# A conditioning step computed in two row halves of the TensorE array, and a reordered GpSimd queue

## The chip, the cores and the metric

The kernel runs on one core of one Trainium2 chip. The metric is the device time of one execution in microseconds (us), the median of three runs. The engines are named as in the profile: PE is TensorE (PEld its weight loads), DVE is VectorE, ACT is ScalarE, POOL is GpSimd, SP is SyncE, which here only issues DMAs.

## The reference, cut to what matters

`x` is 32 batches x 32 tokens x 256 features. The first step conditions it: each batch `b` picks a 32x32 matrix and a bias row by its index, and the matrix mixes the 32 tokens.

```
w = weights[subjects]; b = bias[subjects]          # 32 x (32 x 32), 32 x 32
out = jnp.einsum('bct,bcd->bdt', x, w)             # c, d: the 32 tokens; t: the 256 features
out = out + b[:, :, None]
x = x + attention(out, W_qkv, b_qkv, W_out, b_out) # 16 heads, causal
x = x + ffn(lora_ffn(x, ...), W1, W2, W3)          # gate/up/down with adapters, then an FFN with a
                                                   # Walsh-Hadamard transform folded into W2
```

## The kernel before, in words

**Numbers in two parts.** All large products are made of three matmuls in a rounded 32-bit format: high part times high part, low times high, high times low (`both`, lines 383 to 392). So every activation has a `_hi` copy, written by ACT, and a `_lo` copy, the rest, written by DVE or POOL. A product may start only when both copies are there.

**Halves.** The 1024 tokens are two halves `s` of 16 batches. A half is 4 groups `g` of 128 tokens, and a group is 4 batches of 32 tokens, called slots. Features are two chunks `c` of 128.

**The condition step.** DVE builds it in three instructions for each half: `condition_product` (line 880), `condition_sum` (line 886), which leaves each batch's matrix in `cond_sel`, and `condition_blocks` (line 892), which spreads it to a block matrix of 128 x 128 for each group (four 32x32 blocks on the diagonal, zeros elsewhere), 512 columns for a half. `condition_bias` (line 902, two instructions) writes the bias rows. PE then multiplies, for a half and a feature chunk, four groups of 128x128 by 128 columns in plain f32 (`conditioned`, line 406), which the profile shows as two instructions each, and adds the bias by two matmuls with 8 rows (`conditioned_bias`, line 413). Each pair (s, c) has a PSUM bank. ACT copies the bank to `act_hi` (`conditioned_hi`, line 667), DVE writes `act_lo` and so frees the bank (`conditioned_lo`, line 914). `query`, `key` and `v` read both, and wait for chunk 0 ahead of their first three matmuls and for chunk 1 ahead of the next three (line 421).

**Order.** Each engine has its program written out by hand, in order; nothing is planned at run time. On PE: 14 warm-up matmuls, (0,0) with bias, (0,1) with bias, (1,0), (1,1), the two biases of half 1, then `query(0, 0)`, `key(0, 0)` and the rest. On ACT: two weight splits, `conditioned_hi(0, 0)`, then `fold_raw_hi(0, 1, 2)` (line 748), which waits for the DMA of W2, then `conditioned_hi(0, 1)`, `fold_raw_hi(3)`, and half 1. On DVE: the condition step of half 0 and then of half 1, `weights_lo(W_Q)` (line 909), `conditioned_lo(0, 0)`, `conditioned_lo(0, 1)`.

**Later.** The gate/up products of units 0 to 4 are made half by half, those of units 5 to 7 for both halves together. POOL writes the `_lo` parts of the hidden products (`hidden_lo`, line 1179) and of most weights (`weights_lo`, line 1141), and computes the rest of the Hadamard transform of W2 in six `butterflies` (line 1160). In the loop at line 1224, POOL does for m = 0, 1, 2 two butterflies, then `hidden_lo(1, m)` and one `weights_lo`; for m = 3, 4 only the last two. ACT waits for all six butterflies (line 835), writes the high part of the new W2 in four instructions (line 837), and only then goes on with the SiLU of the gates of unit 5 (`gate`, line 737), which frees PSUM banks that PE claims again for unit 7.

Of the kernel before, what the change touches and what calls it, by code (L numbers as in the profile page):

```python
# [47 lines left out]
BH = B // HALVES  # L48
SLOTS = P // T
GROUPS = BH // SLOTS  # L50
DC = D // P
# [6 lines left out]
N, R = 8, 16  # L58
# [13 lines left out]
C_SLOT = C_ODD + 2  # L72
# [8 lines left out]
W_Q, W_K, W_V, W_OUT, W_A, W_GU = 0, 1, 2, 3, 4, 5  # L81
# [28 lines left out]
ALONE = 5  # L110
# [59 lines left out]
def build(nc, index, first, x_slots, w_stream, matrices, w2_t, x_feat, out):  # L170
    with ExitStack() as ctx:
        def sb(name, shape, dt=F32):
            return ctx.enter_context(nc.sbuf_tensor(name, shape, dt))

        def sem(name):
            return ctx.enter_context(nc.semaphore(name))


        const = sb("const", [P, C_END])
# [4 lines left out]
        ones = sb("ones", [N, P], F32R)  # L184
# [25 lines left out]
        act_hi = sb("act_hi", [P, DC, TOK], F32R)  # L210
        act_lo = sb("act_lo", [P, DC, TOK], F32R)
# [4 lines left out]
        q_t, k_x, v_tok, prob, h_hi, h_lo = [], [], [], [], [], []  # L216
# [14 lines left out]
        x_slot = [k[:, 0:GROUPS * D].rearrange("p (g d) -> p g d", d=D) for k in flat_k]  # L231
        cond_prod = [k[:, 1024:2048].rearrange("p (g d n) -> p g d n", d=T, n=N) for k in flat_k]
        cond_all = const[:, C_COND:C_COND + T * N].rearrange("p (d n) -> p d n", n=N)
        fside = const[0:N, C_FSIDE:C_FSIDE + T]
        cond_blk = prob[1][:, 0:2].rearrange("p i r k -> p (i r k)").rearrange("p (g j d) -> p g j d", j=SLOTS, d=T)

        fb_hi, fb_lo = (w[0:N, RING - TOK:RING].rearrange("p (b d) -> p b d", d=T) for w in (w_hi, w_lo))
        idx_slot = index_f[:, 0:NG]
# [2 lines left out]
        slot_of_pair = const[:, C_ODD:C_ODD + 2]  # L241
# [30 lines left out]
        blk_made = sem("blk_made")  # L272
# [4 lines left out]
        xc_hi_made = sem("xc_hi_made")  # L277
# [23 lines left out]
        def tile(name, s, m):  # L301
            return banks[TILES[name, s, m][0]]

        def wait_full(eng, name, s, m):
            bank, before = TILES[name, s, m]
            eng.wait_ge(bank_full[bank], before + 1)

        def full(ins, name, s, m):
            ins.then_inc(bank_full[TILES[name, s, m][0]], 1)

        def free(ins, name, s, m):
            ins.then_inc(bank_free[TILES[name, s, m][0]], 1)

        def wait_read(eng, name, s, m):

            bank, before = TILES[name, s, m]
            eng.wait_ge(bank_free[bank], before + 1)
# [8 lines left out]
        def half(s):  # L326
            return slice(s * HT, (s + 1) * HT)
# [5 lines left out]
        def y_part(s, i, h):  # L333

            return tile("y", s, i)[:, h * 2 * P:(h + 1) * 2 * P].rearrange("p (g n) -> p g n", g=GROUPS)

        def f32(ap):
            return ap.bitcast(F32)

# [28 lines left out]
        def _(pe):  # L368
            def claim(name, s, m):
                bank, before = TILES[name, s, m]  # L370
                if before:
                    pe.wait_ge(bank_free[bank], before)
                return banks[bank]

            def weights(n):
                wait_weights(pe, n)
                at = PLACES[n][0]
                return w_hi[:, at:at + COLS[n]], w_lo[:, at:at + COLS[n]]
# [19 lines left out]
                return [(h_hi[s][:, k, :], h_lo[s][:, k, :]) for s in ss]  # L398


            def conditioned(s, c):
                ps = claim("xc", s, c)
                pe.wait_ge(blk_made, s + 1)
                pe.wait_ge(x_loaded[s], 16)
                for g in range(GROUPS):
                    pe.matmul(ps[:, g * P:(g + 1) * P], x_slot[s][:, g, c * P:(c + 1) * P],  # L406
                              cond_blk[:, s * GROUPS + g], start=(g == 0), stop=False, skip_group_check=True)

            def conditioned_bias(s, c):
                pe.wait_ge(ones_made, 1)  # L410
                pe.wait_ge(fbias_made, 2 * (s + 1))
                for fb in (fb_hi, fb_lo):
                    last = pe.matmul(tile("xc", s, c)[:, :], ones[:, :], fb[:, s * BH:(s + 1) * BH, :], start=False,  # L413
                                     stop=fb is fb_lo, skip_group_check=True)
                full(last, "xc", s, c)

            def projected(name, n, s, m):
                w = weights(n)
                ps = claim(name, s, m)
                for c in range(DC):  # L420
                    wait_read(pe, "xc", s, c)
                    last = both([ps], unit(w, m * DC + c), rows(act_hi, act_lo, c, [s]), c == 0, c == DC - 1)
                full(last[0], name, s, m)

# [5 lines left out]

            def v(s, j):
                w = weights(W_V)
                for c in range(DC):
                    wait_read(pe, "xc", s, c)
                ps = claim("v", s, j)
                for g2 in range(2):
                    for c in range(DC):
                        at = s * HT + (2 * j + g2) * P
                        x_hi, x_lo = act_hi[:, c, at:at + P], act_lo[:, c, at:at + P]
                        wv = [a[:, c * D:(c + 1) * D] for a in w]  # L440
                        o = ps[:, g2 * D:(g2 + 1) * D]
                        pe.matmul(o, x_hi, wv[0], start=(c == 0), stop=False)  # L442
                        pe.matmul(o, x_hi, wv[1], start=False, stop=False)  # L443
                        last = pe.matmul(o, x_lo, wv[0], start=False, stop=(c == DC - 1))  # L444
                full(last, "v", s, j)
# [88 lines left out]
            pe.wait_ge(warm_made, 1)  # L534
            for _ in range(WARM_UP):
                pe.matmul(banks[7][:, :], warm[:, 0:P], warm[:, :], start=True, stop=True)
            conditioned(0, 0)
            conditioned_bias(0, 0)
            conditioned(0, 1)
            conditioned_bias(0, 1)  # L540
            conditioned(1, 0)
            conditioned(1, 1)
            conditioned_bias(1, 0)
            conditioned_bias(1, 1)
            query(0, 0)
# [60 lines left out]
            for name, n in (("d0", W_D0), ("zd", W_AD), ("d1", W_D1)):  # L606
                w = weights(n)
                tiles = down[name] = [claim(name, s, 0) for s in range(HALVES)]
                for k in range(HC):
                    pe.wait_ge(prod_split, SPLIT_COUNT["up", 1, k])  # L610
                    last = both(tiles, unit(w, k), h_rows(k), k == 0, name == "zd" and k == HC - 1)
# [5 lines left out]
            for s in range(HALVES):  # L617
                for m, name in enumerate(("d0", "d1")):
                    last = both([down[name][s]], unit(w, m), rows(aux_hi, aux_lo, 0, [s]), False, True)
# [18 lines left out]
            for js in ([0, 1], [2], [3], [4]):  # L638
                tiles = [claim("w2", j, 0) for j in js]
                for k in range(HC):  # L640
                    pe.wait_ge(prod_split, SPLIT_COUNT["f3", 1, k])
                    m = OUTS[js[0]][0]
# [3 lines left out]
                    last = both(outs, w, xs, k == 0, k == HC - 1)  # L646
# [5 lines left out]
        def _(act):  # L652
# [9 lines left out]
                act.activation(w_hi[:, at:at + COLS[n]], raw[:, n % STAGES, 0:COLS[n]], ACT.Copy)\  # L662
                   .then_inc(w_hi_made, 1)

            def conditioned_hi(s, c):
                wait_full(act, "xc", s, c)
                act.activation(act_hi[:, c, half(s)], tile("xc", s, c)[:, :], ACT.Copy).then_inc(xc_hi_made, 1)

            def queries(s, m):
                wait_full(act, "q", s, m)  # L670
# [194 lines left out]
        def _(dve):  # L865
# [23 lines left out]
            def condition_blocks(s):  # L889
                g = slice(s * GROUPS, (s + 1) * GROUPS)  # L890
                dve.wait_ge(sel_made, s + 1)
                dve.tensor_tensor(cond_blk[:, g], cond_sel[:, g].unsqueeze(2)
                                  .to_broadcast([P, GROUPS, SLOTS, T]),
                                  const[:, C_SLOT:C_SLOT + SLOTS].unsqueeze(1).unsqueeze(3)
                                  .to_broadcast([P, GROUPS, SLOTS, T]), ALU.mult).then_inc(blk_made, 1)

            def condition_bias(s):
                b = slice(s * BH, (s + 1) * BH)
# [10 lines left out]
                dve.tensor_tensor(w_lo[:, at:at + COLS[n]], raw[:, n % STAGES, 0:COLS[n]],  # L909
                                  f32(w_hi[:, at:at + COLS[n]]), ALU.subtract).then_inc(w_lo_first, 1)  # L910

            def conditioned_lo(s, c):
                dve.wait_ge(xc_hi_made, DC * s + c + 1)
                free(dve.tensor_tensor(act_lo[:, c, half(s)], tile("xc", s, c)[:, :],
                                       f32(act_hi[:, c, half(s)]), ALU.subtract), "xc", s, c)

            def constants():
                dve.tensor_tensor(k_bias[:, :, :], const[:, B_K:B_K + DC].unsqueeze(2).to_broadcast([P, DC, 4]),
# [218 lines left out]
        def _(pool):  # L1137
            def weights_lo(n):
                at = PLACES[n][0]
                pool.wait_ge(w_hi_made, n + 1)  # L1140
                pool.tensor_tensor(w_lo[:, at:at + COLS[n]], raw[:, n % STAGES, 0:COLS[n]],  # L1141
                                   f32(w_hi[:, at:at + COLS[n]]), ALU.subtract).then_inc(w_lo_made, 1)
# [38 lines left out]
            def hidden_lo(s, m):  # L1181
                product_lo("up", s, m, h_hi[s][:, m, :], h_lo[s][:, m, :])
# [39 lines left out]
                    .then_inc(w2_split, 1)  # L1222

            for m in range(ALONE):
                if m < 3:
                    butterflies(m, 0)
                    butterflies(m, 1)
                hidden_lo(1, m)
                weights_lo(W_GU + ALONE + 1 + m)
            for m in range(ALONE, HC):  # L1230
                for s in range(HALVES):
                    hidden_lo(s, m)
# [97 lines left out]
```

## Time and profile before

| | |
|---|---|
| median of 3 runs (lowest to highest) | 228.37 us (228.34 to 228.37) |
| the profiled execution's own time | 228.32 us |
| its span, first to last instruction | 226.5 us |
| PE busy | 220.4 us (97%) |
| DVE, ACT, POOL busy | 85.1, 100.7, 121.8 us |
| mean granted TensorE clock | 0.999 |
| share of the chain that ended last | PE 94%, DVE 3%, DMA 1% |

The span leaves out 1.82 us of the execution's own time. The busy times are those of one execution; a matmul's duration in the rows includes its way through the array, so that neighbours overlap, and what a stream of matmuls costs is the distance between their starts.

### The profile page before, as it was taken

Reading aid. Unit: us, or ns where it says so; the run is one execution under the profiler, and the core shown is the slowest. Engines: PE = TensorE matmul, PEld = TensorE weight load, DVE = VectorE, ACT = ScalarE, POOL = GpSimd, SP = SyncE. Lnnn points to the kernel's source line nnn. Section 1 sums busy time; section 2 is a strip of 40 time slices with the busy share of each in tenths; the row PEclk is TensorE's granted clock in tenths of the full one; section 3 lists DMA queues with packets and bytes.
Section 4 is the critical chain, followed back from the end, with each engine's and each line's share of the span. In section 5 each row is a group of like instructions: output and inputs, shape, how many; then the busy total and the mean of one; then the engine's idle time right before and its main releaser. Section 6 shows DMA issues by size and latency. Waiting matters only on the chain.

```text
span 226.5 us, 3702 instructions
## 1 busy us (share of the span) xinstructions
PE 220.4 (97%) x1482; PEld 179.5 (79%) x1482; DVE 85.1 (38%) x142; ACT 100.7 (44%) x169; POOL 121.8 (54%) x93
## 2 busy tenths in 40 slices
PE   7699999999999999999999999999999999999995
PEld 2477788878888888888888888888888888888894
DVE  4997998898444432211022000202222222220211
ACT  2389799895853324756143000313355555440000
POOL 1039676637787297999993800270266667443000
PEclk9999999999999999999999999999999999999999
DMA  6955400004024000230110000031101100000211
GB/s 182 419 210 177 139 4 3 4 3 139 3 69 138 27 0 8 86 93 26 46 46 0 0 3 0 0 94 45 49 2 50 42 0 3 1 0 0 80 62 46
DMA packets 5345, 13.02 MB, mean 57 GB/s; under 512 B 720, under 2 KB 1360, under 8 KB 5072
## 3 DMA queue, kind: packets, MB, share of 16 engines
q1 hardware_dynamic: 4896, 11.72, 16.6%
q10 hardware_dynamic: 432, 1.07, 1.3%
q8 instruction: 12, 0.20, 0.4%
q14 instruction: 5, 0.04, 0.1%
HBM read 11.73 MB, written 1.05 MB: 56 GB/s over the span
## 4 chain that ended last, share of the span: by engine, by line
PE 94%; DVE 3%; DMA 1%; issue 0%; DVEq 0%
PE bank L387 28%; PE bank L391 28%; PE bank L389 28%; PE bank L463 3%; PE bank L488 2%; DMA index_i<-index 1%; DVE cond_sel L886 1%; DVE k_x L880 1%; PE bank L442 1%; PE bank L406 1%; PE bank L444 1%; PE bank L443 1%; PE bank L472 1%; PE bank L453 1%; PE bank L413 0%
## 5 line engine op out<-in xcount | busy, mean ns | idle before, releaser
L1179 POOL TENSOR_TENSOR h_lo<-tmp_b,h_hi 128x512 fp32r<-128x512 f32 x32 | 41.0, 1299 | 30.5 <-ACT h_hi L727 26.3
L387 PE MATMUL bank<-act_hi,w_hi 128*128 128x512 f32 x152 | 52.8, 392 | 0.1
L391 PE MATMUL bank<-act_hi,w_lo 128*128 128x512 f32 x152 | 52.4, 390 | 0.0
L389 PE MATMUL bank<-act_lo,w_hi 128*128 128x512 f32 x152 | 52.4, 389 | 0.0
L1025 DVE TENSOR_TENSOR tmp_b<-bank,tmp_a 128x512 f32<-128x512 f32 x32 | 21.1, 688 | 73.6 <-PE bank L391 56.2
L1141 POOL TENSOR_TENSOR w_lo<-raw,w_hi 128x512 fp32r<-128x512 f32 (+3 forms) x22 | 35.8, 1638 | 10.2 <-ACT w_hi L662 10.2
L387 PEld LDWEIGHTS bank<-act_hi,w_hi 128*128 128x128 f32 x152 | 28.5, 188 | 6.9 <-issue 1.1
L391 PEld LDWEIGHTS bank<-act_hi,w_lo 128*128 128x128 f32 x152 | 28.5, 188 | 6.1
L389 PEld LDWEIGHTS bank<-act_lo,w_hi 128*128 128x128 f32 x152 | 28.6, 188 | 5.8
L727 ACT ACTIVATE h_hi<-tmp_b 128x512 fp32r<-128x512 f32 x32 | 19.8, 632 | 28.4 <-DVE tmp_b L1025 28.4
L391 PE MATMUL bank<-h_hi,w_lo 128*128 128x512 f32 (+1 forms) x88 | 27.4, 370 | 0.0
L389 PE MATMUL bank<-h_lo,w_hi 128*128 128x512 f32 (+1 forms) x88 | 27.3, 370 | 0.0
L387 PE MATMUL bank<-h_hi,w_hi 128*128 128x512 f32 (+1 forms) x88 | 27.3, 370 | 0.0
L737 ACT ACTIVATE tmp_a<-bank 128x512 f32<-128x512 f32 x32 | 18.0, 595 | 20.7 <-PE bank L391 20.7
L662 ACT ACTIVATE w_hi<-raw 128x512 fp32r<-128x512 f32 (+3 forms) x25 | 18.1, 733 | 5.5 <-DMA raw<-w_stream 5.5
L389 PEld LDWEIGHTS bank<-h_lo,w_hi 128*128 128x128 f32 x88 | 16.6, 188 | 2.8
L387 PEld LDWEIGHTS bank<-h_hi,w_hi 128*128 128x128 f32 x88 | 16.6, 188 | 2.8
L391 PEld LDWEIGHTS bank<-h_hi,w_lo 128*128 128x128 f32 x88 | 16.6, 188 | 2.8
L387 PE MATMUL bank<-aux_hi,w_hi 128*128 128x512 f32 x44 | 16.3, 392 | 0.0
L391 PE MATMUL bank<-aux_hi,w_lo 128*128 128x512 f32 x44 | 16.2, 390 | 0.0
L389 PE MATMUL bank<-aux_lo,w_hi 128*128 128x512 f32 x44 | 16.2, 389 | 0.0
L1160 POOL TENSOR_TENSOR w_fold<-w_fold 128x1024 f32<-128x1024 f32 x6 | 15.3, 2571 | 0.0
(86 smaller groups left out, 245.2 us busy)
## 6 DMA issues: line engine op xcount, KB each, us to landing
raw<-w_stream SPq DMA_DIRECT2D x13, 256.0 KB, 2.7
raw<-w_stream SPq DMA_DIRECT2D x8, 384.0 KB, 3.2
raw<-w_stream SPq DMA_DIRECT2D x3, 512.0 KB, 3.6
k_x<-x_slots ACTq DMA_DIRECT2D x2, 512.0 KB, 6.4
tmp_b<-w_t SPq DMA_DIRECT2D x1, 1024.0 KB, 8.7
resid<-x_feat SPq DMA_DIRECT2D x1, 1024.0 KB, 10.7
out_feat<-tmp_b SPq DMA_DIRECT2D x3, 256.0 KB, 2.1
out_feat<-tmp_b SPq DMA_DIRECT2D x2, 128.0 KB, 1.8
```

The source lines that it names most:

```text
L387: pe.matmul(ps[:, :], w[0], x_hi, start=start, stop=False)
L389: pe.matmul(ps[:, :], w[0], x_lo, start=False, stop=False)
L391: last.append(pe.matmul(ps[:, :], w[1], x_hi, start=False, stop=stop))
L463: last = pe.matmul(tiles[i][32 * j:32 * j + 32, g * 4 * T:(g + 1) * 4 * T], q_t[s][q, c, b * T:(b + 1) * T], k_x[s][q, c, b], start=False, ...
L488: last = pe.matmul(o, v_tok[s][rows_, g, c * P + 32 * i:c * P + 32 * i + 32], prob_t[s][rows_, QUADS * c + i // 2, at:at + 2].rearrange("p ...
L662: act.activation(w_hi[:, at:at + COLS[n]], raw[:, n % STAGES, 0:COLS[n]], ACT.Copy)\
L727: act.activation(dst, tmp_b[:, ORDINAL[name, s, m] % 4, :], ACT.Copy).then_inc(prod_hi_made, 1)
L737: free(act.activation(tmp_a[:, n % 4, :], tile(name, s, m)[:, :], ACT.Silu), name, s, m)
L1025: free(dve.tensor_tensor(tmp_b[:, ORDINAL[name, s, m] % 4, :], tile(name, s, m)[:, :], tmp_a[:, silus % 4, :], ALU.mult), name, s, m)
L1141: pool.tensor_tensor(w_lo[:, at:at + COLS[n]], raw[:, n % STAGES, 0:COLS[n]], f32(w_hi[:, at:at + COLS[n]]), ALU.subtract).then_inc(w_lo_m ...
L1160: pool.tensor_tensor(b[:, t], a[:, 0], a[:, 1], ALU.subtract if t else ALU.add)\
L1179: pool.tensor_tensor(lo, tmp_b[:, n % 4, :], f32(hi), ALU.subtract).then_inc(prod_split, 1)
```

## The change

The 128 rows of a group are taken as two row halves `h` of 64 (two batches each). The block matrix has two 32-column blocks for each row half instead of four: 256 columns for a half `s` and not 512. Each former matmul of 128 rows by 128 columns becomes two of 64 rows by 64 columns, one in each row half of the array, and each row half writes a bank of its own. A bank then holds both feature chunks of the batches of one row half, where it held one chunk of all batches. `conditioned_hi`, `conditioned_lo` and the bias go by `h` for that reason, with addresses in pieces of 64 elements, and the products wait for both banks ahead of their first matmul. In POOL's loop the butterflies come behind `hidden_lo` and `weights_lo`.

```diff
-        cond_blk = prob[1][:, 0:2].rearrange("p i r k -> p (i r k)").rearrange("p (g j d) -> p g j d", j=SLOTS, d=T)
+        cond_blk = prob[1][:, 0:1].rearrange("p i r k -> p (i r k)").rearrange("p (g e d) -> p g e d", e=2, d=T)
...
+        def slot_pair(x, s, h):
+            return x[:, :, half(s)].rearrange("p c (g h n) -> p h c g n", g=GROUPS, h=2)[:, h]
+        def slot_pair_bank(ps):
+            return ps[:, :].rearrange("p (c g n) -> p c g n", c=DC, g=GROUPS)
...
-            def conditioned(s, c):
-                ps = claim("xc", s, c)
+            def conditioned(s):
+                tiles = [slot_pair_bank(claim("xc", s, h)) for h in range(2)]
                 pe.wait_ge(blk_made, s + 1)
                 pe.wait_ge(x_loaded[s], 16)
-                for g in range(GROUPS):
-                    pe.matmul(ps[:, g * P:(g + 1) * P], x_slot[s][:, g, c * P:(c + 1) * P],
-                              cond_blk[:, s * GROUPS + g], start=(g == 0), stop=False, skip_group_check=True)
+                for c in range(DC):
+                    for g in range(GROUPS):
+                        for h in range(2):
+                            rows_ = slice(64 * h, 64 * h + 64)
+                            pe.matmul(tiles[h][:, c, g], x_slot[s][rows_, g, c * P:(c + 1) * P],
+                                      cond_blk[rows_, s * GROUPS + g], start=(c == 0 and g == 0), stop=False,
+                                      skip_group_check=True)
...
             def projected(name, n, s, m):
                 w = weights(n)
                 ps = claim(name, s, m)
+                for h in range(2):
+                    wait_read(pe, "xc", s, h)
                 for c in range(DC):
-                    wait_read(pe, "xc", s, c)
                     last = both([ps], unit(w, m * DC + c), rows(act_hi, act_lo, c, [s]), c == 0, c == DC - 1)
...
-            conditioned(0, 0)
+            conditioned(0)
             conditioned_bias(0, 0)
-            conditioned(0, 1)
             conditioned_bias(0, 1)
-            conditioned(1, 0)
-            conditioned(1, 1)
+            conditioned(1)
...
-            def conditioned_hi(s, c):
-                wait_full(act, "xc", s, c)
-                act.activation(act_hi[:, c, half(s)], tile("xc", s, c)[:, :], ACT.Copy).then_inc(xc_hi_made, 1)
+            def conditioned_hi(s, h):
+                wait_full(act, "xc", s, h)
+                act.activation(slot_pair(act_hi, s, h), slot_pair_bank(tile("xc", s, h)), ACT.Copy)\
+                   .then_inc(xc_hi_made, 1)
...
                 dve.tensor_tensor(cond_blk[:, g], cond_sel[:, g].unsqueeze(2)
-                                  .to_broadcast([P, GROUPS, SLOTS, T]),
-                                  const[:, C_SLOT:C_SLOT + SLOTS].unsqueeze(1).unsqueeze(3)
-                                  .to_broadcast([P, GROUPS, SLOTS, T]), ALU.mult).then_inc(blk_made, 1)
+                                  .to_broadcast([P, GROUPS, 2, T]),
+                                  slot_of_pair.unsqueeze(1).unsqueeze(3)
+                                  .to_broadcast([P, GROUPS, 2, T]), ALU.mult).then_inc(blk_made, 1)
...
             for m in range(ALONE):
+                hidden_lo(1, m)
+                weights_lo(W_GU + ALONE + 1 + m)
                 if m < 3:
                     butterflies(m, 0)
                     butterflies(m, 1)
-                hidden_lo(1, m)
-                weights_lo(W_GU + ALONE + 1 + m)
```

The order of the calls on ACT and DVE is unchanged.

## Rows read from the trace of the kernel before

**Rows 1.** The page: busy us of each engine, share of the span, instructions.
```profile
PE 220.4 (97%) x1482; PEld 179.5 (79%) x1482; DVE 85.1 (38%) x142; ACT 100.7 (44%) x169; POOL 121.8 (54%) x93
```
**Rows 2.** The waits of PE, the longest: us in total, times, longest one.
```profile
PE bank L406 <- DVE prob L892: 2.0, 2, 1.4
```
**Rows 3.** The timeline of PE, 11 to 15 us: start, us, operation, count.
```profile
11.54 2.05 PE L406 MATMUL bank<-prob,k_x 128*128 128x128 f32 x16 [0.57 <-DVE prob L892]
...
13.52 0.50 PE L413 MATMUL bank<-w_hi,ones 8*128 8x512 f32 x1
...
14.33 0.39 PE L413 MATMUL bank<-w_lo,ones 8*128 8x512 f32 x1
14.65 0.50 PE L387 MATMUL bank<-act_hi,w_hi 128*128 128x512 f32 x1
```
**Rows 4.** The timeline of DVE, 6 to 15 us.
```profile
6.49 0.69 DVE L892 TENSOR_TENSOR prob<-cond_sel,const 128x512 f32<-128x512 f32 x1
...
10.79 0.69 DVE L892 TENSOR_TENSOR prob<-cond_sel,const 128x512 f32<-128x512 f32 x1
...
13.21 0.67 DVE L914 TENSOR_TENSOR act_lo<-bank,act_hi 128x512 fp32r<-128x512 f32 x1
14.23 0.69 DVE L914 TENSOR_TENSOR act_lo<-bank,act_hi 128x512 fp32r<-128x512 f32 x1 [0.36 <-ACT act_hi L667]
```
**Rows 5.** The timeline of ACT, 12 to 14.2 us.
```profile
12.05 1.67 ACT L748 ACTIVATE w_hi<-tmp_b 128x512 fp32r<-128x512 f32 x3 [2.19 <-DMA tmp_b<-w_t]
13.62 0.57 ACT L667 ACTIVATE act_hi<-bank 128x512 fp32r<-128x512 f32 x1
```
**Rows 6.** Line 1132 on DVE, both its sizes: durations in ns, min/median/max.
```profile
L1132 DVE TENSOR_TENSOR tmp_b<-bank,resid x5: 425/680/692, 212.5 to 223.9; 128x512 f32<-128x512 f32 x3, 128x256 f32<-128x256 f32 x2
```
**Rows 7.** The timeline of PE's weight loads, from four narrow windows.
```profile
11.54 1.86 PEld L406 LDWEIGHTS bank<-prob,k_x 128*128 128x128 f32 x16 [1.01 <-DVE prob L892]
...
13.52 0.18 PEld L413 LDWEIGHTS bank<-w_hi,ones 8*128 8x128 f32 x1
13.63 0.19 PEld L413 LDWEIGHTS bank<-w_lo,ones 8*128 8x128 f32 x1
...
21.16 0.15 PEld L463 LDWEIGHTS bank<-k_x,q_t 64*32 64x32 f32 x8 [0.23 <-issue]
...
35.75 0.18 PEld L488 LDWEIGHTS bank<-k_x,v_tok 64*32 64x32 f32 x16 [0.36 <-issue]
```
**Rows 8.** The DMAs of x_slots: from issue (1.2 and 1.7 us) to landing.
```profile
DMA to landing us min/median/max: 5.4/6.4/7.5
```
**Rows 9.** Two ACT copies out of PSUM: written in pieces, and in one piece.
```profile
L678 ACT ACTIVATE k_x<-bank,k_bias,const x12: 760/770/784, 17.8 to 33.4; 128x512 f32<-128x512 f32 x12
...
L671 ACT ACTIVATE q_t<-bank,const x4: 682/683/690, 16.6 to 37.3; 128x512 f32<-128x512 f32 x4
```
**Rows 10.** The timeline of POOL, 79 to 107 us.
```profile
79.47 5.73 POOL L1160 TENSOR_TENSOR w_fold<-w_fold 128x1024 f32<-128x1024 f32 x2
...
89.42 4.78 POOL L1160 TENSOR_TENSOR w_fold<-w_fold 128x1024 f32<-128x1024 f32 x2
...
105.53 1.32 POOL L1179 TENSOR_TENSOR h_lo<-tmp_b,h_hi 128x512 fp32r<-128x512 f32 x1
```
**Rows 11.** The timelines of ACT and PE, 102 to 115 us.
```profile
102.00 2.19 ACT L837 ACTIVATE w_hi<-w_fold 128x512 fp32r<-128x512 f32 x4
105.08 1.09 ACT L737 ACTIVATE tmp_a<-bank 128x512 f32<-128x512 f32 x2 [0.88 <-PE bank L391]
...
114.56 0.61 PE L387 MATMUL bank<-act_hi,w_hi 128*128 128x512 f32 x2
```
**Rows 12.** Line 1018 on DVE: durations in ns, first and last start.
```profile
L1018 DVE TENSOR_TENSOR aux_lo<-tmp_b,aux_hi x4: 681/691/1203, 54.3 to 82.3; 128x512 fp32r<-128x512 f32 x4
```
**Rows 13.** The warm-up's weight loads, one before each 512-column matmul.
```profile
2.02 0.15 PEld L536 LDWEIGHTS bank<-warm 128*128 128x128 bf16 x1 [0.28 <-issue]
...
4.15 1.18 PEld L536 LDWEIGHTS bank<-warm 128*128 128x128 bf16 x6 [0.27 <-issue]
```

More of the change, by code:

```diff
@@ L398, in h_rows, with conditioned_bias @@
                 return [(h_hi[s][:, k, :], h_lo[s][:, k, :]) for s in ss]
-            def conditioned(s, c):
-                ps = claim("xc", s, c)
+            def conditioned(s):
+                tiles = [slot_pair_bank(claim("xc", s, h)) for h in range(2)]
                 pe.wait_ge(blk_made, s + 1)
                 pe.wait_ge(x_loaded[s], 16)
-                for g in range(GROUPS):
-                    pe.matmul(ps[:, g * P:(g + 1) * P], x_slot[s][:, g, c * P:(c + 1) * P],
-                              cond_blk[:, s * GROUPS + g], start=(g == 0), stop=False, skip_group_check=True)
-            def conditioned_bias(s, c):
+                for c in range(DC):
[5 more added lines that the diff above has]
+                                      skip_group_check=True)
+            def conditioned_bias(s, h):
                 pe.wait_ge(ones_made, 1)
                 pe.wait_ge(fbias_made, 2 * (s + 1))
+                ps = slot_pair_bank(tile("xc", s, h))
                 for fb in (fb_hi, fb_lo):
-                    last = pe.matmul(tile("xc", s, c)[:, :], ones[:, :], fb[:, s * BH:(s + 1) * BH, :], start=False,
-                                     stop=fb is fb_lo, skip_group_check=True)
-                full(last, "xc", s, c)
+                    pair = fb[:, s * BH:(s + 1) * BH, :].rearrange("n (g h e) d -> n h g (e d)", g=GROUPS, h=2)[:, h]
+                    last = pe.matmul(ps, ones[:, :], pair.unsqueeze(1).to_broadcast([N, DC, GROUPS, 2 * T]),
+                                     start=False, stop=fb is fb_lo, skip_group_check=True)
+                full(last, "xc", s, h)
             def projected(name, n, s, m):
@@ L432, in v @@
                 w = weights(W_V)
-                for c in range(DC):
-                    wait_read(pe, "xc", s, c)
+                for h in range(2):
+                    wait_read(pe, "xc", s, h)
                 ps = claim("v", s, j)
@@ L910, in weights_lo, with conditioned_lo @@
                                   f32(w_hi[:, at:at + COLS[n]]), ALU.subtract).then_inc(w_lo_first, 1)
[L912 to L915, printed above, removed]
+            def conditioned_lo(s, h):
+                dve.wait_ge(xc_hi_made, 2 * s + h + 1)
+                free(dve.tensor_tensor(slot_pair(act_lo, s, h), slot_pair_bank(tile("xc", s, h)),
+                                       f32(slot_pair(act_hi, s, h)), ALU.subtract), "xc", s, h)
             def constants():
```

## The prediction

> **What bounds the kernel now.** I read the page's busy shares first: PE is busy for 220.4 us of 226.5 [rows 1]. Then the waits of PE: the longest is for the block matrix of line 892, 2.0 us in two waits [rows 2], and the only other one that is named is for the warm-up's operand. No later wait of PE on another engine is named, so from the first projection on the kernel is a stream of matmuls, and whatever delays or advances `query(0, 0)` at 14.65 [rows 3] moves the end by as much. The question is what starts that matmul, before and after, so the rest is read from the timelines of the first 15 us.
>
> Before, PE gets there as its own last customer. The block matrix of half 1 is ready at 10.79 + 0.69 = 11.48 [rows 4], the 16 matmuls begin at 11.54 (0.06 later), four bias matmuls follow at 13.52, the last at 14.33, and the query at 14.65 [rows 3]. Its operands are no limit: it first needs `act_lo(0, 0)`, done at 13.21 + 0.67 = 13.88, and `act_lo(0, 1)`, done at 14.23 + 0.69 = 14.92 [rows 4], only three matmuls later, at 14.65 + 3 x 0.23 = 15.34 (a stream of 512-column matmuls starts one every 0.23: two of them take 0.61 and one takes 0.39 [rows 3, 11], so 0.22 to 0.23). So the second copy comes after the query has begun, and is covered by those three matmuls with 0.4 us to spare.
>
> **The change, part by part.**
> *The block matrix* has 256 columns. Line 892 takes 0.69 at 512. The nearest rows with both sizes are those of line 1132, 0.425 against 0.68 to 0.69 [rows 6], so it saves 0.265 each time. Bounds: nothing if a smaller one is no faster, 0.345 if time goes by columns alone. The matrices are ready at 7.18 - 0.27 = 6.91 and 11.48 - 0.53 = 10.95. The data lie there: x_slots' first DMA lands at 1.2 + 5.4 = 6.6 [rows 8], 0.3 ahead.
> *The matmuls.* 32 instructions in a half instead of 16, in 16 rounds of two. What does a round take? Before, loads and matmuls both come 0.11 apart: (1.86 - 0.19) / 15 for the loads (0.19 is the length of one) [rows 7]. With 64 columns the streaming half of it shrinks to some 0.055. The load does not. The bias's two loads, with 8 rows but 128 columns, start 0.11 apart (13.52, 13.63) before any matmul holds them up [rows 7], and the two together take 0.30. Eight loads of 64x32, two in each of four tiles, take 0.15 from the first's start to the last's end [rows 7], so there the second of a tile comes well under 0.1 after the first. A load costs by columns, not by rows, and here the 128 columns of x remain: 0.11 each. The two halves of the array load side by side: the values step starts twice as many loads as the scores step, in eight tiles, and is only 0.03 longer (0.18 against 0.15) [rows 7]. So a round is 0.11 and 16 rounds take what 16 instructions took. The halved columns buy nothing on PE; bounds for a round are 0.055 (streaming alone) and 0.22 (loads one after another, below).
> *Switches of tile shape.* The last bias matmul starts at 14.33 and the next stream at 14.65: 0.32 where like follows like at 0.23, and the first one is longer by 0.1 (0.50 against 0.39) [rows 3]. Half 0 goes matmul, bias, matmul, bias before, and matmul, bias now: two switches of some 0.2 less. They end in the wait for the block matrix of half 1: new, half 0 runs from 6.97 for 16 rounds (1.8), then a switch and four biases (14.65 - 13.52 = 1.13, next switch included), and is through at about 9.9, before 10.95.
> *PE ready for the query.* Everything behind the block matrix of half 1 is as long as before and 0.53 (bounds 0 and 0.69) plus the same 0.06 earlier or equal: 14.65 - 0.53 = 14.12 at the latest.
> *The new wait.* Each bank now holds both feature chunks of half the batches, so the query's first matmul needs `act_lo(0, 1)` too. Its chain has nothing in it that the change shortens: ACT stands idle for 2.19 before 12.05, waiting for the DMA of W2, does three copies, writes `act_hi` at 13.62 to 14.19 [rows 5], and DVE follows at 14.23 to 14.92 [rows 4]. What ACT reads there is full long before, at about 10.1. DVE comes out of its queue 0.53 earlier and only waits longer. With the 0.06 that a wait takes to reach PE, the query starts at 14.92 + 0.05 = 14.97, which is 0.32 later than 14.65, though PE has been idle since 14.1. Behind the waiting query stands PE's whole queue.
> *Addresses in pieces.* Both copies are written in runs of 64. Nearest rows: an ACT copy from PSUM in runs of 32 takes 0.77, one in a single run 0.68 [rows 9], and the first also reads its scale from memory; so 0 to 0.09 for ACT, and I put the same on DVE. Bounds for the wait 0.32 to 0.50; below that only if the chain itself moves. I take 0.32, since 0.09 has the scale as its likelier cause.
> *Later dependences.* Key, fold and scores follow the query's results on PE; they shift with it. The split of W_K follows `conditioned_lo(0, 1)` on DVE and keeps its time, 14.92 + 0.67 = 15.6, ahead of the key at 14.97 + 6 x 0.23 = 16.35.
> *POOL's order.* The first `hidden_lo(1, m)` waits for its operand until after the first butterflies today, so nothing on PE gains from having it first. But POOL now idles where it did butterflies (79.5 to 85.2 [rows 10]) and makes them up later. From 89.42 on a pair of butterflies takes 4.78, and the places of `hidden_lo` and `weights_lo` stay for m = 1 and 2; the last pair comes where the fourth `hidden_lo` starts now, 105.53, and ends at 110.3 [rows 10] instead of 102.0, where ACT now begins its copies [rows 11]. ACT waits for it, then needs 2.19 for the W2 copies and 1.09 for the two gates that PE's unit 7 claims: 113.6. PE claims them at 114.56 [rows 11]. So the wait is 8 us longer on ACT and costs nothing, with 0.9 left; both sides shift by the same 0.32. `hidden_lo` and the weights behind it are 4.8 later than today, and are read by PE from 122 on.
>
> Here a page bears on the margin. Line 1018, a DVE subtraction of two SBUF operands, takes 1.20 at worst where it usually takes 0.69 [rows 12], and the butterflies of that stretch 5.73 a pair against 4.78 [rows 10]. The Trainium skill (SBUF — State Buffer, section "SBUF: two separate sides") says that a DVE instruction with two SBUF inputs and a GpSimd one exclude each other for the whole instruction. By that rule the moved butterflies stay at 4.78, as DVE runs nothing with two SBUF inputs between 89 and 110, which lowers the chance of the third rival; the sum stays.
>
> **Sum.** 226.50 + 0.32 = 226.82 of span, with the 1.82 around it 228.64 beside the profiled execution's 228.32. That one lies 0.05 under the median of the runs, 228.37, so I say 228.7.
>
> **The rivals.**
> 1. *The other side, faster: the W2 DMA lands early.* If ACT is through with the three copies and `act_hi` by 13.3, that is if W2 lands by 11.15 and not at 12.05, DVE's two copies run back to back from 12.7 to 14.0 and PE starts at 14.1: 0.55 saved, 227.8. Before, such an early landing would not show in the time, PE being the bound. For it: the new kernel's DMAs are the same, but its traffic could fall otherwise. Against: 0.9 us in a queue that nothing changed. Chance 0.05.
> 2. *The halves load one after another*, so the rows don't do what the diff says. 32 loads x 0.11 = 3.5 in a half. Half 0: 6.97 to 10.5, bias and switches to 11.8; half 1 to 15.3, bias, query at 16.7: 2.0 later, 230.4. Against it stand the eight tiles of the values step, though each of those loads only 32 columns. Chance 0.06.
> 3. *Butterflies late.* If the six cost 5.73 a pair in their new places, 3 x 0.95 = 2.85 is lost, 0.9 is there, PE stands for 1.9 at unit 7: 230.6. Chance 0.04.
> 4. *The clock.* PE now idles three times before 15 us (5.8 to 7.0, 9.9 to 11.0, 14.1 to 15.0), and works half-filled rounds between. The mean granted clock of the run was 0.999, that is 2.4 GHz. The warm-up shows that matmuls can come slower: loads 0.43 apart up to 4.15 (2.02 and on), then (1.18 - 0.15) / 5 = 0.21 [rows 13]. A second stretch of slow matmuls as long as the first, 1.19 to 4.15, would cost half of it, 1.5: 230.2. Chance 0.04.
>
> **How the numbers follow.** The forecast has 0.75, the rivals 0.19, and 0.06 is for small things of either sign. A measurement can tell 0.2%, 0.46 us, from no change: the forecast's 0.32 is under it, its upper bound over it. Of the 0.75 I put 0.58 within and 0.17 above (copies slower by their bound, or W2 landing a little later, now uncovered). Same: 0.58 + 0.03. Slower: 0.17 + 0.14 + 0.02. Faster: 0.05 + 0.01. The range 228.1 to 229.3 leaves out the four rivals, 0.19; its top is the forecast with both copies 0.3 slower, its bottom half of rival 1.
>
> **What would show it.** Right: in the new profile PE waits by name for line 914 (or whatever precedes it) for about 0.9 us ahead of its first L387, which starts at 14.97; line 892 takes 0.42; loads of 64x128 come in pairs 0.11 apart, 16 rounds in 1.8; ACT idles before line 837 until 110.6, and PE's unit 7 follows without a gap. Wrong: a first L387 before 14.6 or after 15.3, rounds of 0.055 or 0.22, or a named wait of PE beyond 100 us.

## The result

| | before | changed |
|---|---|---|
| median, lowest to highest | 228.36 us (228.34 to 228.37, 4 runs) | 230.88 us (230.77 to 231.04, 4 runs) |
| ratio to before | | 1.0099, 95% interval 1.0069 to 1.0128 |
| profiled execution, span | 228.32, 226.5 | 230.82, 229.0 |
| mean granted TensorE clock | 0.999 | 0.985, in all 4 runs |

The change makes the kernel slower by 2.5 us. The forecast was 228.7 with a range to 229.3; the rival with the clock, which had a chance of 0.04, put it at 230.2. A ratio below leaves out runs more than 1.5% above the fastest run of the same kernel, which are 235.27 and 232.61.

The place is seen when the changed kernel's first 22 us are cut into stretches of 2 us. Columns: stretch, its length, PE busy us (instructions), granted clock as a share of 2.4 GHz, DMA share, GB/s.

```profile
6.00:8.00 2.00, 1.42 (x20) 1.00 1.01 394
8.00:10.00 2.00, 2.00 (x22) 1.00 1.10 448
10.00:12.00 2.00, 1.08 (x19) 1.00 0.99 418
12.00:14.00 2.00, 2.00 (x19) 0.52 0.86 325
14.00:16.00 2.00, 2.00 (x5) 0.50 0.32 118
16.00:18.00 2.00, 2.00 (x6) 0.50 0.48 128
18.00:20.00 2.00, 2.00 (x8) 0.78 0.63 190
20.00:22.00 2.00, 2.00 (x10) 1.00 0.64 200
```

From 12 to nearly 19 us the clock is 1.2 GHz. "PE busy" is 2.00 of 2.00 there and hides it: five or six matmuls fill a stretch that holds ten at full clock (the stretch from 20 us).

The timeline of PE in the changed kernel, 6.9 to 19.1 us, answers to [rows 3]:

```profile
6.95 2.00 PE L418 MATMUL bank<-prob,k_x 64*128 64x64 f32 x32 [0.58 <-DVE prob L907]
...
10.98 2.74 PE L418 MATMUL bank<-prob,k_x 64*128 64x64 f32 x32 [0.92 <-DVE prob L907]
...
13.65 0.79 PE L428 MATMUL bank<-w_hi,ones 8*128 8x512 f32 x1
...
15.10 0.62 PE L428 MATMUL bank<-w_lo,ones 8*128 8x512 f32 x1
...
15.65 0.80 PE L395 MATMUL bank<-act_hi,w_hi 128*128 128x512 f32 x1
16.24 0.63 PE L397 MATMUL bank<-act_lo,w_hi 128*128 128x512 f32 x1
...
18.80 0.44 PE L397 MATMUL bank<-act_lo,w_hi 128*128 128x512 f32 x1
19.07 0.40 PE L399 MATMUL bank<-act_hi,w_lo 128*128 128x512 f32 x1
```

The condition matmuls of half 0 take 2.00 and those of half 1, the same 32, take 2.74, since the clock falls within them. The query starts at 15.65, 1.00 later than at 14.65 [rows 3]. From its first matmul to its ninth it takes 19.07 - 15.65 = 3.42, where eight distances of about 0.23, the first longer by 0.1, are 1.96: 1.46 more. 1.00 + 1.46 = 2.46, and 229.0 - 226.5 is 2.5. So next to nothing is won or lost behind 19.1 us.

How much of the 1.00 would be there at full clock? DVE and ACT of the changed kernel, 6 to 15.3 us, as in [rows 4, 5]:

```profile
6.46 0.43 DVE L907 TENSOR_TENSOR prob<-cond_sel,const 128x256 f32<-128x256 f32 x1
...
10.50 0.42 DVE L907 TENSOR_TENSOR prob<-cond_sel,const 128x256 f32<-128x256 f32 x1
...
12.34 1.67 ACT L763 ACTIVATE w_hi<-tmp_b 128x512 fp32r<-128x512 f32 x3 [2.10 <-DMA tmp_b<-w_t]
13.91 0.58 ACT L681 ACTIVATE act_hi<-bank 128x512 fp32r<-128x512 f32 x1
14.52 0.69 DVE L929 TENSOR_TENSOR act_lo<-bank,act_hi 128x512 fp32r<-128x512 f32 x1 [1.20 <-ACT act_hi L681]
```

The block matrix takes 0.42 to 0.43, as forecast, and the copies in pieces cost nothing (0.58 and 0.69 against 0.57 and 0.69). The W2 data are there at 12.34, not 12.05, so `act_lo` is done at 15.21 and the wait alone would have put the query at 15.26: 0.61 later than before. The slow clock has the other 0.39, and 1.46 behind it: 1.85 us of 2.46. That is a split by calculation. In this execution PE does not stand for `act_lo` at all: the slow clock carries its four bias matmuls past 15.26, and the query follows the last of them, so the two losses lie over each other before 15.65.

### The profile page after: what moved, and what is told of

It is laid out like the page before. It is cut to its first block, busy times and chain, and to the rows that moved or that the text cites. A ratio compares the mean times of both kernels' runs of the same rounds, so it can differ in the third digit from the quotient of the medians.

```text
span 229.0 us, 3769 instructions
## 1 busy us (share of the span) xinstructions
PE 223.6 (98%) x1514; PEld 181.9 (79%) x1514; DVE 84.5 (37%) x142; ACT 100.6 (44%) x169; POOL 120.5 (53%) x93
## 4 chain that ended last, share of the span: by engine, by line
PE 94%; DVE 3%; DMA 1%; issue 0%; DVEq 0%
PE bank L395 28%; PE bank L397 28%; PE bank L399 28%; PE bank L479 3%; PE bank L504 2%; PE bank L418 1%; DMA index_i<-index 1%; DVE cond_sel L901 1%; DVE k_x L895 1%; PE bank L458 1%; PE bank L428 1%; PE bank L459 1%; PE bank L460 1%; PE bank L488 1%; PE bank L469 1%; PE bank L489 0%
## 5 line engine op out<-in xcount | busy, mean ns | idle before, releaser
L395 PE MATMUL bank<-act_hi,w_hi 128*128 128x512 f32 x152 | 53.5, 397 | 0.1
L395 PE MATMUL bank<-aux_hi,w_hi 128*128 128x512 f32 x44 | 16.3, 393 | 0.0
L742 ACT ACTIVATE aux_hi<-tmp_b 128x512 fp32r<-128x512 f32 x6 | 3.8, 633 | 25.9 <-DVE tmp_b L1020 25.8
```

The costliest lines, as they stand in the source:

```text
L395: pe.matmul(ps[:, :], w[0], x_hi, start=start, stop=False)
L742: act.activation(dst, tmp_b[:, ORDINAL[name, s, m] % 4, :], ACT.Copy).then_inc(prod_hi_made, 1)
```

## The experiments

Two theories for the fall of the clock. Theory 1: the half-filled rounds. PE streams 64 columns (0.055 us by the prediction's estimate) behind a weight load of 0.11. "Filled" means 128 columns below, as in the kernel before; no trace shows for how much of its 0.11 us a round keeps the array at work. Theory 2: PE's idle stretches, in the changed kernel's profile at 6.4 (0.58 us) and 10.05 (0.92 us). Every run has its own mean clock, so besides the median it is counted how many runs kept it (mean 0.998 or more). A run whose clock falls has 0.993, 0.985, 0.978 (each to 0.001) or once 0.969. All runs of a comparison were made on the same chip. There were three: the first four runs below on one, the next four on a second, the last three on a third, and the kernel before kept its clock in 22 of 25, 19 of 25 and 20 of 29 runs there.

One thing varies that no edit sets. The same 14 warm-up matmuls take 4.63 us in the profile of the kernel before and 4.76 to 6.07 in the profiles below, since they come 0.43 apart at first and 0.21 apart later, and the turn comes at a different time in each execution. The first idle stretch is what the warm-up leaves: 1.41 in the kernel before, 0.58 in the changed one, and none in some executions. Only one run of each kernel has a trace, so the idle time of the other runs is not known.

**The first four.**

The changed kernel with 128 columns streamed in each 64-row matmul:

```diff
-                            pe.matmul(tiles[h][:, c, g], x_slot[s][rows_, g, c * P:(c + 1) * P],
-                                      cond_blk[rows_, s * GROUPS + g], ...
+                            pe.matmul(tile("xc", s, h)[:, at:at + P], x_slot[s][rows_, g, c * P:(c + 1) * P],
+                                      cond_blk[rows_, pair:pair + 2], ...
```

> The changed kernel, but each of the 64-row matmuls of the condition step streams 128 columns instead of 64 (its window in the bank overlaps the next one's, so the condition step's result is not the reference's; every count, wait and bank stays). The changed kernel's clock falls to half at 12.0 us and returns at 18.8. Theory 1, the half-filled rounds (64 streamed columns behind a 0.11 us weight load) are what lowers the clock: here a round is filled and still takes 0.11, so the clock stays at 1.00 throughout and the time is 228.7 (the exposed wait of 0.32 alone), 228.5 to 229.0. Theory 2, the idle stretches of PE (6.0 to 6.95, 10.05 to 10.98) lower it: they are unchanged here, so the mean clock is 0.985 again and the time 230.9.

Measured: 229.88 (228.80 to 230.91, 10 runs), ratio 1.0055 (1.0025 to 1.0085). Three runs kept the clock (228.80, 228.94, 228.97), six had 0.992 or 0.993, one 0.985. Neither theory alone: filling the rounds helps (0.985 in all four runs of the changed kernel, in 1 of 10 here), but is not enough. In its profile the two idle stretches are 0.95 and 0.87, longer than the changed kernel's, and the clock falls before 12 us all the same, for about half as long.

The kernel before with 64 columns streamed in each 128-row matmul:

```diff
-                    pe.matmul(ps[:, g * P:(g + 1) * P], ..., cond_blk[:, s * GROUPS + g], ...
+                    pe.matmul(ps[:, g * P:g * P + 64], ..., cond_blk[:, s * GROUPS + g, 0:2], ...
```

> The kernel before, but each of the 128-row matmuls of the condition step streams only 64 of its 128 columns (half of the condition step's result is left out). Theory 1: loads hold the distance at 0.11 us, the array streams half the time, the clock falls after 11 us here too, mean clock near 0.985, and the time is 1.5 to 3 us over 228.4. Theory 2: the idle stretches are as in the kernel before (1.4 and 0.6 us), so the clock stays and the time is 228.3 to 228.5.

Measured: 232.84 (232.38 to 232.96, 4 runs), ratio 1.0182 (1.0144 to 1.0220), mean clock 0.978 in all four. Its stretches, same columns:

```profile
8.00:10.00 2.00, 1.82 (x13) 1.00 1.07 433
10.00:12.00 2.00, 1.85 (x7) 0.57 1.03 434
12.00:14.00 2.00, 2.00 (x11) 0.50 0.70 295
...
20.00:22.00 2.00, 2.00 (x9) 0.87 0.77 218
```

And its timeline of PE up to the fall:

```profile
1.19 5.97 PE L536 MATMUL bank<-warm 128*128 128x512 bf16 x14 [1.19 <-DVE warm L867]
7.31 1.10 PE L406 MATMUL bank<-prob,k_x 128*128 128x64 f32 x8
8.60 0.47 PE L413 MATMUL bank<-w_hi,ones 8*128 8x512 f32 x1 [0.18 <-DVE w_lo L902]
...
10.25 0.79 PE L413 MATMUL bank<-w_hi,ones 8*128 8x512 f32 x1
```

With the program and the shapes of its weights as they were, and only half the columns, the kernel before loses its clock in every run. The expectation had the idle stretches at 1.4 and 0.6. In the profiled run the warm-up lasts to 7.16 and the first of them is not there; PE never idles for as much as 0.2 us between 1.19 and the fall at about 10.3, where the bias matmul takes 0.79 and not 0.49. So idle time is not needed for a fall, and neither are the row halves; fewer streamed columns are enough. Whether the row halves add something is not shown.

The changed kernel with the idle stretches filled:

```diff
-WARM_UP = 14
+WARM_UP = 17
...
             conditioned_bias(0, 1)
+            for _ in range(5):
+                pe.matmul(banks[7][:, :], warm[:, 0:P], warm[:, :], start=True, stop=True)
             conditioned(1)
```

> The changed kernel with 17 warm-up matmuls instead of 14 and five more of them between the biases of half 0 and the condition matmuls of half 1, so that PE does not idle at 6.0 to 6.95 and 10.05 to 10.98. Theory 2 (idle stretches): the clock stays at 1.00, time 228.7 to 229.0. Theory 1 taken strictly (half-filled rounds alone suffice): mean clock 0.985, 230.9. If what counts is the sum of streaming work, the filler also holds the clock up, so a full clock here and in the run with 128 streamed columns would say that either cure works.

Measured: 230.55 (228.79 to 231.95, 10 runs), ratio 1.0083 (1.0042 to 1.0124); three runs kept the clock (228.79, 228.98, 229.10). Filling the first two idle stretches keeps the clock as often as filling the rounds does, and is not enough either; three runs have 0.984 or 0.985 and are at 231.74 to 231.95, above the changed kernel. In its profiled run the clock is 0.98 from 14 to 16 us and 0.50 from 16 to 18: it falls behind the third idle stretch (0.84), the one that the new wait makes. The edit also adds streaming work, so it does not test idle time alone, and it holds up PE: half 1's condition matmuls start at 11.39 and not 10.98.

The kernel before with the new wait:

```diff
                 for c in range(DC):
                     wait_read(pe, "xc", s, c)
+                for c in range(DC):
                     last = both([ps], unit(w, m * DC + c), ...
```

> The kernel before, with query and key waiting for both chunks of the conditioned activations ahead of their first matmul, as the changed kernel does. Forecast's step: the query starts at 14.97 instead of 14.65, clock full, time 228.36 + 0.32 = 228.7. Rival: the wait is hidden, 228.36; or it adds enough idle time for the clock to fall, 230 and more.

Measured: 229.02 (228.54 to 229.84, 10 runs), ratio 1.0024 (1.0006 to 1.0041), clock kept in 9 of 10. The wait by itself costs 0.2 to 0.8 in the runs that kept the clock, 0.7 in the median, against the kernel's 228.35. In its profile the query starts at 15.42:

```profile
12.40 1.67 ACT L749 ACTIVATE w_hi<-tmp_b 128x512 fp32r<-128x512 f32 x3 [2.45 <-DMA tmp_b<-w_t]
...
15.42 0.47 PE L387 MATMUL bank<-act_hi,w_hi 128*128 128x512 f32 x1 [0.62 <-DVE act_lo L915]
```

The W2 copies start at 12.40 here, and the chain behind them is the forecast's. The spread of the runs is likely the landing of that DMA, which the kernel before covers; only the profiled run shows where it landed. The new wait does not bring the clock down here. The changed kernel with filled rounds has the same wait and kept its clock in only 3 of 10 runs: the two still differ in the row halves and in the order of half 0, which makes the second idle stretch 0.87 and not about 0.6. Which of the two tells was not tested.

**The other order on GpSimd, alone in the kernel before** (the last hunk of the change, nothing else):

> The kernel before with only the order of GpSimd's loop changed, hidden_lo and weights_lo ahead of the butterflies. Forecast's step: ACT waits some 8 us for the last butterflies, PE waits for nothing, 228.35, the same as before. Rival: the later low parts or the late gates cost something that the changed kernel hides behind its slow clock, 228.8 or more.

Measured: 228.33 (228.27 to 229.93, 10 runs), ratio 0.9989 (0.9963 to 1.0014), clock kept in 9 of 10. No difference. ACT's wait is there, and PE does not notice:

```profile
110.40 2.20 ACT L837 ACTIVATE w_hi<-w_fold 128x512 fp32r<-128x512 f32 x4 [8.49 <-POOL w_fold L1160]
```

**The wait taken out of the changed kernel**, by ACT's order:

```diff
-            fold_raw_hi(0, 1, 2)
             conditioned_hi(0, 1)
+            fold_raw_hi(0, 1, 2)
             fold_raw_hi(3)
```

> The changed kernel, with ACT's copy of the second bank of half 0 ahead of the three W2 copies that wait for the DMA. The new wait is gone: the query can start when its biases are through, about 14.1 at full clock. If the wait were the larger part of the loss, 228.4 or less. If the clock is (theory 1: half-filled rounds), it still falls at about 12 us in most runs: mean clock 0.985 and 230 to 230.9. My count for the changed kernel: of 2.5 us some 0.6 are the wait, hidden inside the slow stretch, the rest the clock; so I expect 230.3 to 230.9 here.

Measured: 232.15 (230.82 to 232.34, 4 runs), ratio 1.0155 (1.0126 to 1.0184), clock 0.978 in three and 0.985 in one. Slower still than the changed kernel, by more than I expected: the slow stretch is longer.

```profile
10.00:12.00 2.00, 1.28 (x13) 0.81 1.00 422
12.00:14.00 2.00, 2.00 (x24) 0.50 0.87 333
14.00:16.00 2.00, 2.00 (x8) 0.50 0.33 118
16.00:18.00 2.00, 2.00 (x5) 0.50 0.48 136
18.00:20.00 2.00, 2.00 (x6) 0.50 0.69 197
20.00:22.00 2.00, 2.00 (x7) 0.63 0.67 198
```

Why the clock comes back at about 21 here and at 19 in the changed kernel, with the same stream of matmuls, stays open. It is clear that the wait was not what lowered it: the clock falls before 12 us, and the wait would come at 14.

**The same, with the idle stretches filled** (17 warm-ups and five matmuls, as above):

> The same order on ACT, and the filling matmuls of the earlier run (17 warm-ups, five between the biases of half 0 and half 1). If streaming work in the first 15 us decides, the last idle stretch (14.5 to 15.4, where the clock fell in the earlier run) is gone as well, and more runs than 3 of 10 hold the full clock; at full clock the query starts at about 14.6, 228.3. Half-filled rounds alone sufficient: clock 0.985 or 0.993 in most runs, 229.5 to 231.

Measured: 228.61 (227.94 to 235.27, 10 runs), ratio 1.0003 (0.9977 to 1.0029), clock kept in 7 of 10. The clock still falls in 3 of 10, once very far (0.969, 235.27). Its profile, of a run that kept the clock, shows that one idle stretch can be left: the 17 warm-ups took only 5.21 there, and PE stood for 0.83 before 7.24, for the DMA of `x_slots`. So this run does not show half-filled rounds without idle time; the one that does is the kernel before with half the columns.

**And the rounds filled too** (128 columns of data):

> As the run before, and each condition matmul streams 128 columns in place of 64 (the condition step's result is not the reference's). No idle stretch and no half-filled round is left, so by theory 1 and by theory 2 every run holds the full clock, and the time is 228.2 to 228.5. If some runs still fall, something else than PE's streaming work sets the clock.

Measured: 228.24 (227.99 to 228.77, 10 runs), ratio 0.9993 (0.9976 to 1.0009), clock kept in 10 of 10. Against 7 of 10 with half-filled rounds this alone would be too few runs to tell.

**A version with the reference's result.** The 64 columns lie beside 64 columns of zeros, written once at the start by GpSimd. A matmul streams both, and the zeros are added to the neighbouring window of the bank:

```diff
+            pool.memset(cond_zero, 0.0).then_inc(zero_made, 1)
...
+                            n = c * GROUPS + g
+                            at = (n - 1) * 64 if n else 0
+                            col = (s * GROUPS + g) * P + (0 if n else 64)
+                            pe.matmul(tile("xc", s, h)[:, at:at + P], x_slot[s][rows_, g, c * P:(c + 1) * P],
+                                      cond_zb[rows_, col:col + P], start=(n == 0), stop=False, ...
```

With ACT's order, 15 warm-ups and three filling matmuls:

> A version with the reference's result meant to beat both: the changed kernel, each condition matmul streams its 64 columns beside 64 columns of zeros that are added to the neighbouring window (a round is filled and still 0.11 us), ACT's second copy ahead of the W2 copies, 15 warm-ups, three filling matmuls between the halves. If filled rounds and no idle stretch hold the clock (10 of 10 in the run with 128 streamed columns of data), every run is at full clock; the condition matmuls of half 1 start at about 11.0 and not 11.8, the query at 14.1, 227.7 to 228.1. Rival: streamed zeros don't count as work for the clock, and it falls in some runs as with 64 columns (7 of 10 held there), up to 231.

Measured: 227.86 (227.78 to 228.07, 12 runs), ratio 0.9956 (0.9935 to 0.9977), clock kept in 12 of 12. It is faster than both kernels: 0.55 under the median of the kernel before, which was 228.41 in this comparison (0.5 under its runs at full clock). PE's timeline shows what the change had meant to bring, and rounds that cost no more for their zeros (2.06 against 2.00 and 2.05 [rows 3]):

```profile
7.12 2.06 PE L425 MATMUL bank<-prob,k_x 64*128 64x128 f32 x32
...
11.08 2.06 PE L425 MATMUL bank<-prob,k_x 64*128 64x128 f32 x32
13.06 0.49 PE L435 MATMUL bank<-w_hi,ones 8*128 8x512 f32 x1
...
14.19 0.50 PE L398 MATMUL bank<-act_hi,w_hi 128*128 128x512 f32 x1
```

14.19 is 0.46 ahead of 14.65, and the span is 226.0 where it was 226.5.

**The same without filling matmuls:**

> The same without any filling matmul (14 warm-ups, nothing between the halves): against the changed kernel with ACT's order alone (232.15, clock down in 4 of 4) it differs only in the zeros streamed. Theory 1, the half-filled rounds were the cause: the clock falls in few runs, as in the run with 128 data columns (3 of 10 held, 6 fell for a short stretch, 1 for a long one) or better, since the last idle stretch is gone; median 228 to 229.5. If idle stretches are the cause the clock falls as before, 231 to 232.

Measured: 227.86 (227.74 to 232.61, 12 runs), ratio 0.9989 (0.9954 to 1.0023), clock kept in 8 of 12. Against the run with ACT's order alone (0 of 4, 232.15) the zeros, with their `memset` and one wait for it, are the whole difference of the edits. The comparison goes across two chips, and the executions that were profiled differ in the first idle stretch, 0.38 here and 1.14 there, which the warm-up and the DMA of `x_slots` set; the second is 0.87 against 0.72.

**The kernel before with filling alone** (17 warm-ups, two matmuls between the halves):

> The kernel before with filling only: 17 warm-ups, and two matmuls between the biases of half 0 and the condition matmuls of half 1. The kernel before fell to the half clock in 9 of 50 runs, at 229.8 to 230.0. Filled idle stretches should take these runs away: all runs at full clock, 228.3 to 228.5. Rival: a fall that idle time does not cause stays in about one run of five.

Measured: 228.38 (228.27 to 228.71, 12 runs), ratio 0.9975 (0.9953 to 0.9997), clock kept in 12 of 12. That filling takes away the falls of the kernel before too is likely, at 20 of 29 without it on the same chip.

Runs that kept the clock, of the runs above:

| rounds of the condition step | no filling matmuls | with filling matmuls |
|---|---|---|
| changed kernel, 64 columns | 0 of 4 | 3 of 10 |
| changed kernel, 128 columns of data | 3 of 10 | |
| changed kernel with ACT's order, 64 columns | 0 of 4 | 7 of 10 |
| changed kernel with ACT's order, 128 columns of data | | 10 of 10 |
| changed kernel with ACT's order, 64 columns and 64 of zeros | 8 of 12 | 12 of 12 |
| kernel before, 128 columns | 61 of 79 | 12 of 12 |
| kernel before with the new wait, 128 columns | 9 of 10 | |
| kernel before with the other order on GpSimd, 128 columns | 9 of 10 | |
| kernel before, 64 columns | 0 of 4 | |

Wherever two cells differ only in the streamed columns or only in the filling, the clock holds more often with more streaming. Single pairs, such as 7 of 10 and 10 of 10, are too few runs to tell; the table as a whole is not. A filling matmul both ends an idle stretch and adds streaming work, so the table does not part idle time from the amount of work; the kernel before with 64 columns shows that the amount matters where there is no idle time.

## Why the prediction was wrong

The step that failed is in the sum. It has a term for the new wait and none for the clock, which stood at full speed throughout. The clock was low from 12.1 to 18.9 us, and that is 1.85 of the 2.46 us. The second failure is of size: the wait's term was 0.32, and 0.61 was there.

*What bounds the kernel*: right. The start of the query moves the end by as much; 2.46 us are lost before 19.1 us and none later.

*A round is 0.11 because the load costs by columns*: right, and the two halves do load side by side (rival 2 is out). 32 loads take what 16 took, 1.86 [rows 7]:

```profile
6.94 1.86 PEld L418 LDWEIGHTS bank<-prob,k_x 64*128 64x128 f32 x32 [1.07 <-DVE prob L907]
```

*"The halved columns buy nothing on PE"*: this is where the term for the clock was put at nothing. As PE time the sentence holds. But I took a round that is held by its load as neutral, and it is not: the array streams half as much, and the clock goes. Rival 4 names it ("works half-filled rounds between") together with the idle stretches, and has 0.04 on no more than the mean clock of one run of the kernel before, 0.999. That row could not show how near the edge the kernel before stood: 18 of its 79 later runs fell. The idle stretches that rival 4 lists were no longer than before: ahead of the fall PE waited 0.58 + 0.92 = 1.50 in the changed kernel, and 1.41 + 0.57 = 1.98 in the kernel before. The price of rival 4, 1.5, was near the measured 1.85 by luck. It was half of one slow stretch of 2.96 us; the slow stretch was 6.8 us, and a part of what it cost is hidden behind the wait for `act_lo`.

*The new wait*: the mechanism was right, the term too small. 0.32 was counted from one execution, in which the W2 copies started at 12.05; in the twelve other profiles they start between 12.19 and 12.54, and the wait alone costs 0.7 in the median (229.02), 0.6 by the changed kernel's profile. The sign that was named for it, PE waiting by name for `act_lo`, is in the profile of the kernel before with the wait (0.62), and not in that of the changed kernel. A DMA's landing in one execution was taken as its landing in all. At full clock the changed kernel would have been at about 228.9 (three runs with filled rounds: 228.80 to 228.97).

*The block matrix* (0.265 saved each, measured 0.26), *copies in pieces* (nothing): right.

*POOL's order*: right to 0.1 us. The last butterflies ended at 110.3 + 2.5, ACT stood for 8.5, PE for nothing. Of the changed kernel, as in [rows 10, 11]:

```profile
91.95 4.77 POOL L1175 TENSOR_TENSOR w_fold<-w_fold 128x1024 f32<-128x1024 f32 x2
...
108.03 4.75 POOL L1175 TENSOR_TENSOR w_fold<-w_fold 128x1024 f32<-128x1024 f32 x2
...
112.81 2.19 ACT L852 ACTIVATE w_hi<-w_fold 128x512 fp32r<-128x512 f32 x4 [8.54 <-POOL w_fold L1175]
114.91 1.06 ACT L752 ACTIVATE tmp_a<-bank 128x512 f32<-128x512 f32 x2
...
117.09 0.61 PE L395 MATMUL bank<-act_hi,w_hi 128*128 128x512 f32 x2
```

The pairs stay at 4.75 to 4.77 where no DVE instruction with two SBUF inputs runs, as the rule of the Trainium skill (SBUF — State Buffer, section "SBUF: two separate sides") had it. Rival 3 is out.

*Rival 1* (an early W2): did not occur. ACT's order takes the wait away as an early landing would, and with the clock held it gave 227.86 where I had worked out 227.8.

*Slips.* By its own terms rival 2 comes to 10.5 + 1.13 + 3.5 + 1.13 = 16.3 for the query and not 16.7, so to 230.0 and not 230.4. "The data lie there, 0.3 ahead" was one execution too: in two later profiles half 0's condition matmuls wait for the DMA of `x_slots`, to 7.09 and 7.24.

## What to carry to other kernels

Before packing small matmuls into parts of the array, ask what a round is held by. If it is the weight load, fewer streamed columns save no time and lower the array's work, and in a kernel's first microseconds, where the engine also waits, this cost the clock of the 7 us that followed, and up to 10. Look at the granted clock of every run, not of one profile: the kernel before showed 0.999 in its profile and fell in 18 of 79 runs. Streaming zeros beside a load that sets the pace cost nothing here (2.06 against 2.05 for the 128 columns of the kernel before). Filling matmuls in a waiting stretch are free only while they end before the wait does: three put off the next condition matmuls by 0.1 us at most, five by 0.4.

## What the runs showed of the hardware that was not expected

- A PE that the profile calls busy can still lose its clock. With 64 columns and no filling it fell in 12 of 12 runs of three kernels. The idle stretches of PE between warm-up and fall were 0.58 and 0.92 us in one profile, 1.14 and 0.72 in the second and under 0.2 in the third, the kernel before with half the columns. The Trainium skill (TensorE: Matmul & The Clock Gate, section "HAM oscillation — how this bites in real kernels") explains a falling clock by idle stretches between bursts. The third profile does not agree: the streaming inside a burst counts as well.
- Zeros count as work for the clock: 20 of 24 runs that streamed them kept it. 8 of the 12 among them without filling did, against 0 of 4 of the same kernel without zeros and without filling.
- The granted clock of the profile does not show the slow start. It reads 1.00 from 0 to 6 us in every profile here, though the warm-up's matmuls come 0.43 apart for the first 3 to 5 us and 0.21 apart afterwards. So a mean of 0.999 does not speak of that time.
- The length of a fall varies between kernels that differ little: the clock was low to about 19 us in the changed kernel and to about 21 us with another order on ACT. This was not settled.
